# Conditioning products for two tiles at a time, x and result in one ring of four buffers, in a two-layer adapter kernel

## The chip, the cores and the metric

The kernel runs on one core of a Trainium2 chip. The metric is device time in microseconds (us), lower is better. The core has TensorE (in the rows PE, its weight loads PEld), VectorE (DVE), ScalarE (ACT), GpSimd (POOL) and SyncE (SP), which here issues every DMA. All engines run their own program and meet at semaphores.

## The reference

```python
def cond0(x, weights, condition):                 # 128 samples, 64 channels, 1024 columns
    return jnp.einsum('bct,bcd->bdt', x, weights[condition])     # one 64x64 matrix a sample
def ffn0(x, W_base, b_base, W_router, A, B):      # 8 experts of rank 16, best 2, scale 2
    probs = softmax(x @ W_router.T); top2, idx = top_k(probs, 2); top2 /= top2.sum(-1, keepdims=True)
    combine = einsum('nk,nke->ne', top2, one_hot(idx, 8))
    hw = einsum('nd,erd->ner', x, A) * combine[:, :, None]
    return x @ W_base.T + b_base + einsum('ner,eor->no', hw, B) * 2
def cond1(x, ids, W, b, A, B):                    # one of 32 adapters of rank 16 a sample
    return x @ W.T + b + einsum('bsr,bor->bso', einsum('bsd,brd->bsr', x, A[ids]), B[ids])
def ffn1(x, w, bias, s_in, s_w):                  # both operands rounded to fp8 first
    return einsum('ni,io->no', fp8(x / s_in), fp8(w / s_w)) * (s_in * s_w) + bias
x = x + ffn0(cond0(x, ...), ...)
x = x + ffn1(cond1(x, ...), ...)
```

## The kernel before

The 8192 rows are 64 tiles of 128 rows, two samples a tile. The kernel has two stages with a loop over the 64 tiles in each; every engine has its own copy of the loops, and the order of its instructions is the order in which the Python code writes them.

**Stage 1**, some 15 us a tile. TensorE works in three PSUM banks g = 0, 1, 2 (`bank_g`), eight k-steps of 128 rows in each; every float32 product is made of three matmuls with the operands split in a high and a low part (`st_h`, `st_l`, `w0h`, `w0l`), so a tile has 72 of them (lines 977 to 979). Bank 0 also holds the adapters' and the router's columns. Behind bank 1 stands the *conditioning product* of the next tile (`cond`, line 957): 16 matmuls with 64 rows and 32 columns of weights each, from `wpair` (two 64x64 matrices) and `xbuf` (the next tile's x) into `bank_f`. Behind bank 2 nine matmuls add the experts' part (lines 1004 to 1006), for which VectorE must have made `hwt` out of bank 0 (softmax, best two, a transpose, 12 small casts at line 317 with ScalarE doing 4 more). Then the next tile follows.

VectorE transposes the conditioned tile from `bank_f` to `bank_t` in two halves (`turn_y`, line 727), ScalarE rounds each half to `st_h` (`st_hi`, line 624) once TensorE has read the old one (`st_used`, raised at half and at the end of bank 2), and VectorE subtracts (`st_lo`, line 733) to `st_l`. It adds x and stores the result to `x1buf` (line 831) and a block-transposed copy to `x1_blocks` (line 840). GpSimd adds the bias row to `xbuf` (`add_bias`, line 547).

x and result have two buffers each (`xbuf`, `x1buf`). SyncE's order in a tile: first `feed(t)`, which for three pieces of the second stage's tables (40 pieces in all) waits for GpSimd's `split` (`pool_lo`), stores the two parts and loads the next piece; then `tile(t)`: wait for the result, store it, load x of tile t+2 and its two matrices (`load_cond`, with a value loaded from `ids0_sb` for each), store the four blocks. ScalarE and VectorE quantize one piece of `wq` in each of the tiles 2 to 33. TensorE's loop body is two tiles (tiles 2 to 61); the other engines write tiles 0 to 33 out.

Ahead of tile 0, 26 pieces of the stage's weights come in through 12 staging slots (8 in `wq`, 4 in `x1buf`) and are split by ScalarE and VectorE (lines 630, 743), which also serves tile 0's operands behind piece 1.

**Stage 2**, some 15 us a tile: the same three banks with 72 matmuls (lines 1030 to 1032), three for the adapters' second part and the bias (line 1075, operand `b_stack`), and 16 bf16 matmuls for the quantized product of the tile before (line 1040). ScalarE and VectorE make `st_h` and `st_l` of the transposed tile read back from DRAM (`turned_hi`, line 676; `turned_lo`, line 882). `turned_hi` waits for `main_done`, the end of bank 2 of the tile before. The bias rows are split on chip between the stages (`bias_h`, `bias_l`) and copied into both `b_stack`.

## Time and profile before

| | us |
|---|---|
| median of 3 runs | 2020.85 (2020.4 to 2025.44) |
| profiled execution, its own time | 2019.35 |
| its span | 2017.5 |
| TensorE busy | 1983.1 (98%) |
| VectorE busy | 1490.1 (74%) |
| GpSimd busy | 517.5 (26%) |
| ScalarE busy | 393.9 (20%) |

The span is the stretch that the trace covers, all times in its rows count from its start. Stage 1 ends near 1014 us, stage 2 takes the rest. In the rows an engine's "idle before" is followed by what released it. PEclk is the clock granted to TensorE, 1.00 for 2.4 GHz and 0.50 for 1.2 GHz.

### The profile page before, as it was taken

Reading aid. Unit: us, or ns where it says so; the run is one execution under the profiler, and the core shown is the slowest. Engines: PE = TensorE matmul, PEld = TensorE weight load, DVE = VectorE, ACT = ScalarE, POOL = GpSimd, SP = SyncE. Lnnn points to the kernel's source line nnn. Section 1 sums busy time; section 2 is a strip of 40 time slices with the busy share of each in tenths; the row PEclk is TensorE's granted clock in tenths of the full one; section 3 lists DMA queues with packets and bytes.
Section 4 is the critical chain, followed back from the end, with each engine's and each line's share of the span. In section 5 each row is a group of like instructions: output and inputs, shape, how many; then the busy total and the mean of one; then the engine's idle time right before and its main releaser. Section 6 shows DMA issues by size and latency. Waiting matters only on the chain.

```text
span 2017.5 us, 38464 instructions
## 1 busy us (share of the span) xinstructions
PE 1983.1 (98%) x13056; PEld 1802.5 (89%) x13056; DVE 1490.1 (74%) x3882; ACT 393.9 (20%) x1084; POOL 517.5 (26%) x469
## 2 busy tenths in 40 slices
PE   6899999999999999999999999999999999999998
PEld 5889999999999999999988888888888888888887
DVE  6887877777766666666657777777777777777777
ACT  3112111111211111111112121212121222122211
POOL 3655411111111111111112222322232223222222
PEclk8999999999999999999999999999999999999999
DMA  7764443343333333333455566566656665665564
GB/s 241 226 192 140 135 122 107 104 126 116 101 111 110 98 97 116 106 96 113 123 162 151 163 166 161 152 168 164 163 148 173 160 161 149 173 159 161 155 171 111
DMA packets 220202, 289.93 MB, mean 144 GB/s; under 512 B 97795, under 2 KB 169477, under 8 KB 220166
## 3 DMA queue, kind: packets, MB, share of 16 engines
q1 hardware_dynamic: 220166, 289.56, 50.7%
q14 instruction: 27, 0.22, 0.0%
q8 instruction: 9, 0.15, 0.0%
HBM read 163.62 MB, written 109.05 MB: 135 GB/s over the span
## 4 chain that ended last, share of the span: by engine, by line
PE 93%; SPq 2%; DMA 2%; POOL 1%; DVE 1%; issue 0%; ACT 0%; DVEq 0%; ACTq 0%
PE bank_g L977 13%; PE bank_g L1032 12%; PE bank_g L979 12%; PE bank_g L978 12%; PE bank_g L1031 12%; PE bank_g L1030 12%; PE bank_f L1040 11%; PE bank_f L957 3%; PE bank_g L1075 1%; PE bank_g L1005 1%; PE bank_g L1006 1%; PE bank_g L1004 1%; DMA raw<-b 1%; DMA raw<-a 1%; POOL w1h L557 1%; POOL w1l L559 1%
## 5 line engine op out<-in xcount | busy, mean ns | idle before, releaser
L977 PE MATMUL bank_g<-w0h,st_h 128*128 128x384 f32 (+1 forms) x1536 | 529.7, 345 | 10.4 <-DMA wpair<-wc 6.5
L978 PE MATMUL bank_g<-w0l,st_h 128*128 128x384 f32 (+1 forms) x1536 | 520.7, 339 | 0.0
L979 PE MATMUL bank_g<-w0h,st_l 128*128 128x384 f32 (+1 forms) x1536 | 520.6, 339 | 0.0
L1030 PE MATMUL bank_g<-w1h,st_h 128*128 128x352 f32 x1536 | 506.1, 329 | 4.0 <-DVE st_l L882 4.0
L1032 PE MATMUL bank_g<-w1h,st_l 128*128 128x352 f32 x1536 | 496.7, 323 | 0.0
L1031 PE MATMUL bank_g<-w1l,st_h 128*128 128x352 f32 x1536 | 495.8, 323 | 0.0
L882 DVE TENSOR_TENSOR st_l<-xbuf,st_h 128x512 fp32r<-128x512 f32 x128 | 212.8, 1703 | 183.9 <-ACT st_h L676 183.9
L977 PEld LDWEIGHTS bank_g<-w0h,st_h 128*128 128x128 f32 x1536 | 289.5, 188 | 41.2 <-issue 26.1
L547 POOL TENSOR_TENSOR xbuf<-xbuf,b_base_sb 128x1024 f32<-128x1024 f32 x64 | 154.4, 2412 | 654.0 <-PE bank_f L957 640.4
L1030 PEld LDWEIGHTS bank_g<-w1h,st_h 128*128 128x128 f32 x1536 | 289.2, 188 | 11.9 <-DVE st_l L882 4.6
L1031 PEld LDWEIGHTS bank_g<-w1l,st_h 128*128 128x128 f32 x1536 | 289.0, 188 | 1.6
L978 PEld LDWEIGHTS bank_g<-w0l,st_h 128*128 128x128 f32 x1536 | 289.7, 189 | 0.0
L979 PEld LDWEIGHTS bank_g<-w0h,st_l 128*128 128x128 f32 x1536 | 289.6, 189 | 0.0
L1032 PEld LDWEIGHTS bank_g<-w1h,st_l 128*128 128x128 f32 x1536 | 289.4, 188 | 0.0
L1040 PE MATMUL bank_f<-wq,rqt 128*128 128x512 bf16 x1008 | 228.6, 380 | 0.1
L601 POOL TENSOR_TENSOR obuf<-x1buf,bias_sb 128x1024 f32<-128x1024 f32 x64 | 176.8, 2763 | 153.2 <-DMA out<-obuf 153.2
L582 POOL TENSOR_TENSOR w1h<-raw,ones 128x128 fp32r<-128x128 f32 x128 | 48.7, 402 | 585.5 <-DMA raw<-a_split 546.9
L1040 PEld LDWEIGHTS bank_f<-wq,rqt 128*128 128x128 bf16 x1008 | 93.8, 98 | 112.4 <-issue 0.4
L317 DVE CAST hwt<-hw_parts 32x64 fp32r<-32x64 f32 x768 | 150.4, 196 | 11.8
L733 DVE TENSOR_TENSOR st_l<-bank_t,st_h 128x512 fp32r<-128x512 f32 x128 | 87.7, 686 | 79.3 <-ACT st_h L624 78.9
L831 DVE TENSOR_TENSOR x1buf<-bank_g,xbuf 128x384 f32<-128x384 f32 (+1 forms) x192 | 91.9, 506 | 73.5 <-PE bank_g L1006 73.4
L615 ACT ACTIVATE ht<-h_parts 32x32 fp32r<-32x32 f32 x192 | 43.8, 228 | 488.0 <-DVE h_parts L907 486.5
(79 smaller groups left out, 1988.8 us busy)
## 6 DMA issues: line engine op xcount, KB each, us to landing
xbuf<-x SPq DMA_DIRECT2D x64, 512.0 KB, 3.9
x_scratch<-x1buf SPq DMA_DIRECT2D x64, 512.0 KB, 2.9
x1t_scratch<-x_blocks SPq DMA_DIRECT2D x256, 128.0 KB, 2.3
xbuf<-x1t_scratch SPq DMA_DIRECT2D x64, 512.0 KB, 3.6
x1buf<-x_scratch SPq DMA_DIRECT2D x64, 512.0 KB, 5.1
out<-obuf SPq DMA_DIRECT2D x64, 512.0 KB, 2.7
b_stack<-b_split SPq DMA_DIRECT2D x384, 64.0 KB, 3.6
raw<-a_split SPq DMA_DIRECT2D x128, 128.0 KB, 4.2
```

Of the source, the lines that this page charges most:

```text
L317: last = engine_move(hwt[32 * q:32 * q + 32, :, 32 * a:32 * a + 32], hw_parts[32 * a:32 * a + 32, :, 32 * q:32 * q + 32])
L547: pool.tensor_tensor(xbuf[:, b, :], xbuf[:, b, :], b_base_sb[:, :], ALU.add).then_inc(xb_done, 1)
L601: pool.tensor_tensor(obuf[:, b, :], x1buf[:, b, :], bias2_sb[:, :], ALU.add).then_inc(x1b_done, 1)
L831: dve.tensor_tensor(x1buf[:, b, cols], bank_g[:, g, G0_OUT[g]:G0_WIDTH[g]], xbuf[:, b, cols], ALU.add).then_inc(x1_done[g], 1)
L882: last = dve.tensor_tensor(turned(st_l[:, :], h), in_blocks(xbuf[:, b, :], h), turned(st_h[:, :], h), ALU.subtract)
L977: pe.matmul(to, st_h[:, rows], w0h[:, k, cols], start=(k == 0), stop=False)
L978: pe.matmul(to, st_h[:, rows], w0l[:, k, cols], start=False, stop=False)
L979: last = pe.matmul(to, st_l[:, rows], w0h[:, k, cols], start=False, stop=(k == KC - 1))
L1030: pe.matmul(to, st_h[:, rows], w1h_k[:, k, cols], start=(k == 0), stop=False)
L1031: pe.matmul(to, st_h[:, rows], w1l_k[:, k, cols], start=False, stop=False)
L1032: last = pe.matmul(to, st_l[:, rows], w1h_k[:, k, cols], start=False, stop=(k == KC - 1))
L1040: last = pe.matmul(bank_f[:, h, :], rqt[:, k * P:(k + 1) * P], wq[:, k, h * HALF:(h + 1) * HALF], start=(k == 0), stop=(k == KC - 1))
```

## The change

1. TensorE makes the conditioning products of two tiles in one block of 32 matmuls, in every second tile only; the results lie in a PSUM tensor of four banks (`bank_y`). `bank_t` shrinks to one bank, so that the second half is transposed only when the first half has been split.
2. `xbuf` and `x1buf` become `ring`, four buffers; the result takes the place of its x. x of tile t+4 is loaded when the store of result t has landed (`x1_stored`). The loop bodies of TensorE, VectorE, GpSimd and SyncE are four tiles; 36 tiles (TensorE: 4) are written out before them.
3. SyncE does `tile(t)` first and `feed(t)` behind it, with two table pieces a tile. The bias row is one more table piece (41), split by GpSimd and read back from DRAM.
4. At the start x of tile 1 and 2 is loaded between the weight pieces, the bias row `b_base` and x of tile 3 behind them; two of the staging slots lie in `x1_blocks`.
5. Between the stages: VectorE makes `turned_lo` of tile 0 half by half around the last result; in all of stage 2 `turned_hi` goes by `st_used`, half by half; GpSimd fills the adapter columns of tile 1 before it waits for the result and `bias2`.

```diff
-POOL_PIECES_A_TILE = 3
+POOL_PIECES_A_TILE = 2
+RING = 4
+UNROLLED = -(-PREP_TILES // RING) * RING
+def pairs_to(t):
+    return (t + 1) // 2 + 1
...
+        y_of = (bank_y[:, 2:4, :], bank_y[:, 0:2, :])
+        bank_f, bank_l = bank_y[:, 0:2, :], bank_y[:, 2:4, :]
...
                     if n == KC - 1:
-                        sp.dma_start(b_base_sb[:, :], b_base.partition_broadcast(P)).then_inc(b_base_loaded, 16)
...
-                        sp.dma_start(xbuf[:, 1, :], x_t[1]).then_inc(x_loaded[1], 16)
-                        load_cond(1, 1)
+                    if n in (KC + KC // 2 - 1, 2 * KC - 1):
+                        r = 1 if n < 2 * KC - 1 else 2
+                        sp.dma_start(ring[:, r, :], x_t[r]).then_inc(x_loaded[r], 16)
+                        load_cond(r, r)
+                sp.dma_start(b_base_sb[:, :], b_base.partition_broadcast(P)).then_inc(b_base_loaded, 16)
+
+                sp.wait_ge(w0_lo, len(w0_units))
+                sp.dma_start(ring[:, RING - 1, :], x_t[RING - 1]).then_inc(x_loaded[RING - 1], 16)
...
-                    if more:
-                        sp.dma_start(xbuf[:, b, :], x_t[bass.ds(t + 2, 1)].rearrange("a p n -> (a p) n"))\
-                          .then_inc(x_loaded[b], 16)
-                        load_cond(t + 2, b)
...
+                    if more:
+
+                        sp.wait_ge(x1_stored, 16 * (t + 1))
+                        sp.dma_start(ring[:, r, :], x_t[bass.ds(t + RING, 1)].rearrange("a p n -> (a p) n"))\
+                          .then_inc(x_loaded[r], 16)
+                        load_cond(t + RING, r)
...
-                for t in range(PREP_TILES):
+                for t in range(UNROLLED):
+                    tile(t, t % RING, True)
                     feed(t)
-                    tile(t, t % 2, True)
...
-                        act.wait_ge(main_done, t)
                     for h in range(2):
+
+                        act.wait_ge(st_used[h], TILES + t)
...
+                def cond(pair):
+
+                    for r, _ in pair:
+                        for s in range(2):
+                            cols = slice(s * D // 4, (s + 1) * D // 4)
+                            for q in range(4):
+                                for j in range(PER_TILE):
+                                    rows = slice(j * CH, (j + 1) * CH)
+                                    last = pe.matmul(y_of[r % 2][32 * q:32 * q + 32, j, cols],
...
                     last.then_inc(y_ps, 1)
...
+                cond_in([(0, 1)], None)
+                cond([(0, 1)])
+                tile(0, False, [(1, 1), (2, 1)])
+                tile(1, True, ())
+                tile(2, True, [(3, 1), (0, 2)])
+                tile(3, True, ())
+                with pe.Fori(RING, TILES - 2 * RING + 1, RING) as i:
```

On TensorE, at the conditioning product inside tile 1 before the change (lines 977 to 979 are the three matmuls of a k-step of bank 1 and then bank 2), there stands:

```order
L977 MATMUL bank_g<-w0h,st_h 128x384 [waits st_ps1,wc_loaded0,x_loaded0]
L978 MATMUL bank_g<-w0l,st_h 128x384
L979 MATMUL bank_g<-w0h,st_l 128x384
L957 MATMUL bank_f<-xbuf,wpair 32x256 x16
L977 MATMUL bank_g<-w0h,st_h 128x384 [waits x1_done2]
```

In the changed program tile 1 has no such block. Tile 2 has one of twice the length (lines 990 to 992 and 970 are the new numbers of the same matmuls):

```order
L990 MATMUL bank_g<-w0h,st_h 128x384 [waits wc_loaded0,x_loaded0,st_ps1,wc_loaded3,x_loaded3]
L991 MATMUL bank_g<-w0l,st_h 128x384
L992 MATMUL bank_g<-w0h,st_l 128x384
L970 MATMUL bank_y<-ring,wpair 32x256 x32
L990 MATMUL bank_g<-w0h,st_h 128x384 [waits x1_done2]
```

The block moved from every tile to every second one, with x and matrices of two tiles awaited at once. On VectorE, behind the 12 small casts of tile 0, there stands before the change:

```order
L317 CAST hwt<-hw_parts 32x2x32 x11
L727 STREAM_TRANSPOSE bank_t<-bank_f 128x512 [waits y_ps]
L727 STREAM_TRANSPOSE bank_t<-bank_f 128x512
L733 TENSOR_TENSOR st_l<-bank_t,st_h 128x512 [waits hi_done0]
L831 TENSOR_TENSOR x1buf<-bank_g,xbuf 128x256 [waits acc_ps0,xb_done]
L733 TENSOR_TENSOR st_l<-bank_t,st_h 128x512 [waits hi_done1]
```

In the changed program, at the same place:

```order
L327 CAST hwt<-hw_parts 32x2x32 x11
L740 STREAM_TRANSPOSE bank_t<-bank_y 128x512 [waits lo_done1,y_ps]
L746 TENSOR_TENSOR st_l<-bank_t,st_h 128x512 [waits hi_done0]
L740 STREAM_TRANSPOSE bank_t<-bank_y 128x512 [waits lo_done0]
L849 TENSOR_TENSOR ring<-bank_g,ring 128x256 [waits acc_ps0,xb_done]
L746 TENSOR_TENSOR st_l<-bank_t,st_h 128x512 [waits hi_done1]
```

The second transpose moved behind the first subtraction. On SyncE, behind the end of tile 0, there stands before the change (`TENSOR_LOAD` and what follows it is the loading of an index for `load_cond`; the six rows before these are table pieces that wait for `pool_lo`):

```order
L397 DMA a_split<-w1h 128x4x128 [waits pool_lo]
L397 DMA a_split<-w1l 128x4x128
L370 DMA raw<-a 128x4x128
L410 DMA x_scratch<-x1buf 128x1024 [waits x1_done2]
L413 DMA xbuf<-x 128x1024
L348 TENSOR_LOAD ids_sb
```

In the changed program:

```order
L426 DMA x_scratch<-ring 128x1024 [waits x1_done2]
L432 DMA x1t_scratch<-x_blocks 32x4x256 [waits blocks_done]
L432 DMA x1t_scratch<-x_blocks 32x4x256 x3
L437 DMA ring<-x 128x1024 [waits x1_stored]
L358 TENSOR_LOAD ids_sb
```

The table pieces moved behind the tile's own transfers, and the load of x behind the result's store and the blocks.

## Rows read from the trace of the kernel before

**Rows 1.** The page: busy time and its share of the span.

```profile
PE 1983.1 (98%) x13056; PEld 1802.5 (89%) x13056; DVE 1490.1 (74%) x3882; ACT 393.9 (20%) x1084; POOL 517.5 (26%) x469
```

**Rows 2.** Stages: window, its length, busy by engine, PEclk, DMA share, GB/s.

```profile
600.00:800.00 200.00, 200.00 (x1475) 189.43 (x1474) 127.45 (x444) 33.82 (x105) 31.38 (x13) 1.00 0.34 104
1000.00:1200.00 200.00, 195.00 (x1142) 174.59 (x1141) 142.10 (x301) 39.46 (x102) 46.84 (x59) 0.99 0.58 162
...
35.70:41.80 6.10, 6.07 (x20) 6.10 (x21) 4.91 (x8) 1.19 (x2) 6.02 (x4) 0.50 0.73 194
...
1031.30:1035.20 3.90, 3.87 (x14) 3.87 (x15) 3.80 (x5) 0.00 (x0) 0.00 (x0) 0.56 0.84 308
```

**Rows 3.** TensorE in order of time: last matmuls of tiles 0, 5, 62, 63.

```profile
38.11 0.52 PE L1006 MATMUL bank_g<-b0h,hwt 128*128 128x384 f32 x1
...
125.41 0.34 PE L1006 MATMUL bank_g<-b0h,hwt 128*128 128x384 f32 x1
...
999.32 0.34 PE L1006 MATMUL bank_g<-b0h,hwt 128*128 128x384 f32 x1
...
1013.46 0.34 PE L1006 MATMUL bank_g<-b0h,hwt 128*128 128x384 f32 x1
```

**Rows 4.** TensorE in order of time, around one conditioning product.

```profile
501.75 0.34 PE L979 MATMUL bank_g<-w0h,st_l 128*128 128x384 f32 x1
502.02 1.09 PE L957 MATMUL bank_f<-xbuf,wpair 64*32 64x256 f32 x32
503.04 0.44 PE L977 MATMUL bank_g<-w0h,st_h 128*128 128x384 f32 x1
503.32 0.34 PE L978 MATMUL bank_g<-w0l,st_h 128*128 128x384 f32 x1
```

**Rows 5.** Groups by line: busy, mean ns; then that block's records in flight in 0.05 us.

```profile
L957 PE MATMUL bank_f<-xbuf,wpair 64*32 64x256 f32 x2048 | 71.7, 390 | 6.3 <-DMA wpair<-wc 6.3
...
502.25:502.30 0.05, 0.05 (x15) 1.00 0.90 307
```

**Rows 6.** Waits on SyncE and TensorE up to 130 us: total, times, longest.

```profile
SPq L397 <- POOL w1l L559: 31.1, 7, 6.7
...
PE bank_g L1004 <- DVE hwt L317: 6.8, 1, 6.8
PE bank_g L977 <- DMA wpair<-wc: 6.5, 4, 3.0
```

**Rows 7.** TensorE in tile 4; SyncE's largest wait in the whole span.

```profile
100.33 0.69 PE L977 MATMUL bank_g<-w0h,st_h 128*128 128x384 f32 x1 [3.03 <-DMA wpair<-wc]
...
SPq L410 <- DVE x1buf L831: 455.5, 58, 9.3
```

**Rows 8.** VectorE in one tile of the steady state.

```profile
503.35 1.31 DVE L727 STREAM_TRANSPOSE bank_t<-bank_f 128x512 f32<-128x512 f32 x2
506.13 0.69 DVE L733 TENSOR_TENSOR st_l<-bank_t,st_h 128x512 fp32r<-128x512 f32 x1 [1.47 <-ACT st_h L624]
507.99 0.42 DVE L831 TENSOR_TENSOR x1buf<-bank_g,xbuf 128x256 f32<-128x256 f32 x1 [1.17 <-PE bank_g L1006]
```

**Rows 9.** VectorE, the 12 casts to hwt: tile 0, then a steady tile.

```profile
31.87 3.71 DVE L317 CAST hwt<-hw_parts 32x64 fp32r<-32x64 f32 x12
...
501.04 2.39 DVE L317 CAST hwt<-hw_parts 32x64 fp32r<-32x64 f32 x12
```

**Rows 10.** TensorE's idle stretches between the stages.

```profile
1016.30 0.43 PE L1030 MATMUL bank_g<-w1h,st_h 128*128 128x352 f32 x1 [2.50 <-DVE st_l L882]
...
1029.09 0.74 PE L1075 MATMUL bank_g<-b_stack,ht 98*128 98x320 f32 x3 [1.00 <-DMA b_stack<-bias_l]
...
1031.33 0.43 PE L1030 MATMUL bank_g<-w1h,st_h 128*128 128x352 f32 x1 [1.50 <-DVE st_l L882]
```

**Rows 11.** Instruction queue, window 50:100 (packets, MB, share); a DMA of 16 KB, us to landing.

```profile
q8 instruction: 3, 0.05, 0.5%
...
wpair<-wc SPq DMA_DIRECT2D x4, 16.0 KB, 2.1
```

More of the change, by code:

```diff
@@ L774, in quantize_weight, with tile @@
                     dve.tensor_tensor(to, to, wq_nan, ALU.add).then_inc(wq_step, 1)
-                def tile(t, b, stored, blocks, more, piece=None):
+                def tile(t, r, next_pairs, blocks, more, piece=None):
                     n = t + 1
@@ L973, in bank @@
                             pe.wait_ge(w0_lo, w0_need[g] - KC + k + 1)
[L974 to L975 removed]
+                        if pair and k == KC - 1:
+                            cond_in(pair, n)
                         rows = slice(k * P, (k + 1) * P)
@@ L983, in bank, with tile @@
                     return last
-                def tile(t, b, loads, prior, more):
+                def tile(t, prior, pair):
                     n = t + 1
@@ L992, in tile @@
                             pe.wait_ge(x1_done[g], t)
-                        last = bank(g, n, prior, *((loads, 1 - b) if g == 1 and more else ()))
+                        last = bank(g, n, prior, pair if g == 1 else ())
                         if g == 0:
                             last.then_inc(h_ps, 1)
-                        if g == 1 and more:
-                            cond(1 - b)
+                        if g == 1 and pair:
+                            cond(pair)
                     for e in range(2):
```

226 lines of the change are left out of this document (108 added, 118 removed).

## The prediction

> **What bounds the kernel now.** I read the page first: TensorE is busy 98% of the span, the next engine 74% [rows 1]. So the end moves only by what TensorE does or waits for, and the views that count are those of TensorE's idle time and of its order in time. The table of stages shows the steady state of stage 1 without idle time, 200.00 of 200, and 195.00 between 1000 and 1200 us, where the stages meet [rows 2]. The last matmuls of four tiles then measure tiles: tiles 6 to 62 take (999.32 - 125.41)/57 = 15.33 us each; tile 63, the only one without a conditioning product, takes 1013.46 - 999.32 = 14.14; tiles 1 to 5 take 125.41 - 38.11 = 87.3, which is 10.7 more than five steady ones [rows 3]. So there are three sources of gain: the conditioning product (62 x 1.19 us in tiles 1 to 62), the start (10.7), and the seam between the stages. The sum is made against the profiled execution's own 2019.35 us; the median of the runs shown is 1.5 above it.
>
> **The conditioning product.** It costs a tile 15.33 - 14.14 = 1.19 us. The order in time says what of. Main matmuls start 14.14/81 = 0.175 apart; the block starts 0.27 behind the last of them, the next main one 1.02 behind the block's start, and the one after 0.28 later [rows 4]. The 32 records of the block lie in 1.09 us, one takes 0.39, and 15 are in flight 0.23 to 0.28 us after its start [rows 4, 5]. So they come in four waves of 8 (2 row halves by 4 column quarters of the array), the last starting 1.09 - 0.39 = 0.70 after the first, less 0.05 for the issue within a wave: 0.65/3 = 0.22 from wave to wave. The next main matmul starts only when the last wave has nearly run out. A second product right behind the first adds four waves, 4 x 0.215 = 0.86 us, and saves one entry and one exit, 0.33. Bounds: it adds no less than 0.70, the starts of one block, and no more than the whole 1.19.
> Tiles 1 to 63 before hold 62 products: 73.8 us. After, the blocks stand in tiles 0, 2, ..., 62; in tiles 1 to 63 these are 30 pairs and one single: 31 x 1.19 + 30 x 0.86 = 62.7. That is -11.1 us: 9.9 by fewer entries and exits, and one product less since tile 0 takes it on. In tile 0 TensorE waits 6.8 us for hwt anyway [rows 6], so the 0.86 there are covered; without that cover they would be +0.9.
>
> **The second transpose, which moved behind the first subtraction.** VectorE's first subtraction starts at 506.13 and takes 0.69, so the transpose (1.31 for two, 0.68 for the second) now runs from 506.85 to 507.53, in the 1.17 us in which VectorE waited for TensorE before 507.99 [rows 8]. ScalarE rounds the second half only when TensorE is done with bank 2, which is no earlier. Cost nothing; 0.46 us of cover are left ahead of line 831, whose result releases bank 0 of the next tile. In tiles without a block everything on TensorE behind bank 1 comes 1.19 earlier against VectorE's chain to hwt; hwt is ready at 501.04 + 2.39 = 503.43 [rows 9], and line 1004, 23 matmuls behind the one at 503.32 [rows 4], starts at 503.32 + 23 x 0.175 = 507.3, so 3.9 us of slack shrink to 2.7. Cost nothing.
>
> **The ring.** x of tile t+4 now waits for the store of result t, and is needed by a block that stands two tiles later or more. SyncE sat 455.5 us in 58 tiles waiting for a result, 7.9 a tile [rows 7]; its work in a tile is the other 7.4 of 15.3, and the new wait for a store of 512 KB, a few us, fits in what is left. It is hidden, with a tile as margin.
>
> **The start.** SyncE waited seven times for GpSimd's pieces, 31.1 us, before it got to a tile's own loads, and TensorE then waited for the matrices `wpair`, 6.5 us in four stalls [rows 6]; the longest, in tile 4, is 3.03 us [rows 7]. The change puts the pieces behind, and loads four tiles ahead. So the 10.7 us should go, but for what the clock takes: from 35.7 to 41.8 us TensorE ran at 0.50, which is 1.2 GHz, behind the 6.8 us of waiting in tile 0 [rows 2, 6]. That wait stays, so tile 1 still loses about half of the 3.4 us behind 38.4, 1.7. Net -9.0. If two tiles still wait for late loads it is -5.
> Tile 0 itself: the 12 casts took 3.71 against 2.39 in the steady state [rows 9], while GpSimd split table pieces; these now come later, -1.3. Against that the last weight piece is issued later, since SyncE puts x and both matrices of one more tile ahead of it. VectorE's chain to hwt starts behind the last piece; I give 0.8 of the 1.3 back: -0.5, with -3 and +2 as ends.
>
> **The seam.** Three idle stretches, 2.50 + 1.00 + 1.50 = 5.0 us [rows 10], and a clock of 0.56 behind the last, which costs about 1.7 more [rows 2]. `turned_lo` of tile 0 no longer stands behind the last transpose, the bias rows come from DRAM, and `turned_hi` starts at half of bank 2: all three releasers come earlier. What is late next: the six DMAs to `b_stack` of tile 0, which stand behind the same result as before, and bank 0 of stage 2's tile 1, which ScalarE must read out before it is written, with no bf16 matmuls to cover that yet. I take 1.2 of the 6.7 us for both: -5.5, with -3.5 if the clock falls once again. In stage 2 proper TensorE has no idle time to give back, and `turned_hi` earlier by half a bank releases nobody: 0.
>
> **TensorE's longer program.** Its loop body grows from two tiles to four, and 4 tiles stand ahead of it. Here one rule speaks against the change. The rows show three packets of 16 KB on an instruction queue between 50 and 100 us [rows 11], which I read as TensorE's code, about one a tile; from 100 to 1000 us, in the loop, that queue is silent. So the old body, two packets long and so in up to three, with the one ahead of it, is held without a fetch: four packets at least. The new body is four long, so five or six with its ends and the one ahead. Whether that many are held no row shows. I take nothing, since nothing in the trace marks an edge between four and six. The Trainium skill, page "Runtime: NRT & Kernel Launch", section "Instruction fetch mechanics", says two things: that TensorE's instruction memory holds 128 KiB, by which the sum stays as it is, and that it is only two lines, a taken branch out of which stalls for a fetch, by which it would grow at each of the 13 jumps back. The silent queue speaks against two lines.
>
> **Sum.** -11.1 - 9.0 - 0.5 - 5.5 = -26.1: 2019.35 - 26.1 = 1993.3 for a profiled run, and 1.5 more for the median, **1995 us**. The ends of the terms: -11.1 becomes -1.2 if the pair saves nothing and -15.3 with 0.72 for the second product; the others -5, +2 and -3.5 on one side, -10.7, -3 and -7.2 on the other. Not all fall on one side: 1989 to 2003 for this case.
>
> **The rivals.**
> *The pair saves no entry* (each product runs out before the next, since weights for new rows are loaded): 30 x 0.33 = +9.9, 2005. Against it: waves with other weights already follow each other at 0.22 within a block. Chance 0.08.
> *VectorE becomes the bound*: its chain through one `bank_t` releases bank 0 late. From a delay of 0.46 us on each tile pays the excess; two `add_bias` in a row beside it are what could bring it. With 0.3 us on 63 tiles +19, 2014. For it: the cover is the smallest in the kernel. Chance 0.07.
> *SyncE stays late at the start*: a table piece waits for GpSimd, the store behind it, and TensorE again for `wpair`: +8, 2003. Chance 0.09.
> *The jump back stalls* (slower): the loop's first packet is no longer held. Price of one: a DMA of the same 16 KB lands 2.1 us after its issue [rows 11], so 2 to 3 us; 13 jumps give +26 to +39, 2021 to 2034. It decides from 2.0 us a jump on. Chance 0.06.
> The forecast itself has 0.70.
>
> **Chances.** A difference of 0.3%, 6 us, is about what a measurement of this kernel can tell from none. Faster by more: all but the last rival and part of the second, 0.92; within: 0.03; slower: 0.05. The range 1988 to 2006 holds the forecast's own and the two rivals near 2004.
>
> **What the changed profile would show.** The block's record count 64 in every second tile, with next main matmul about 1.89 us behind its start; tiles alternating 14.14 and 16.2 us; tiles 1 to 5 without waits for `wpair`; the stretch 1000 to 1200 with less than 2 us idle; no packets on the 16 KB queue in the loop. The prediction is wrong if TensorE waits on `x1buf`'s line in every tile, or if a gap stands at every fourth tile's start.

## Result: 10.7 us faster, where 26 were predicted

| | before | after |
|---|---|---|
| median | 2021.18 us (5 runs, 2020.4 to 2025.44) | 2010.44 us (5 runs, 2009.63 to 2013.28) |
| profiled execution, its span | 2017.5 us | 2008.1 us |

The ratio is 0.9945, 95% interval 0.9932 to 0.9958. The median lies 4.4 us above the upper end of the predicted range. The page of the changed kernel, its busy times and the costliest group (at its end the idle time before it and what ended most of that):

```profile
PE 1973.0 (98%) x13056; PEld 1809.6 (90%) x13056; DVE 1437.2 (72%) x3881; ACT 400.1 (20%) x1083; POOL 494.7 (25%) x471
...
L990 PE MATMUL bank_g<-w0h,st_h 128*128 128x384 f32 (+1 forms) x1536 | 526.0, 342 | 10.3 <-DVE ring L849 5.4
```

The shares look as in [rows 1]. New is the releaser in the group's last column: TensorE's bank 0 waits for `ring L849`, VectorE's addition that reads a bank and writes the result (line 831 before). To see where the 26 us went, the span is cut at four events, as in [rows 3]: the last matmul of tile 0, of tile 11 and of tile 63, and the last of the three LoRA matmuls (line 1075 before, 1095 after) of stage 2's third tile. "Steady" is 11 x 15.33 = 168.6 us before, and 6 x 14.14 + 5 x 16.20 = 165.8 with pairs.

| | before | after | moved | predicted |
|---|---|---|---|---|
| tile 0 ends at | 38.11 | 40.12 | +2.0 | -0.5 |
| tiles 1 to 11, above steady | 10.6 | 13.0 | +2.4 | -9.0 |
| fewer entries and products: 2.79 in tiles 1 to 11, 8.29 in tiles 12 to 63 (796.08 to 787.79) | | | -11.1 | -11.1 |
| end of stage 1 to the third LoRA block | 46.84 | 44.60 | -2.2 | -5.5 |
| rest of stage 2, to the end | | | -0.4 | 0 |
| sum before rounding, against spans of 2017.5 and 2008.1 | | | -9.4 | -26.1 |

So one term was exact and three failed. TensorE's waits of over 0.1 us between 40 and 215 us in the changed kernel (total, times, longest):

```profile
PE bank_g L990 <- DVE ring L849: 5.4, 6, 1.4
PE bank_g L1017 <- DVE hwt L327: 3.7, 3, 2.1
```

and the two longest up to 41 us, the first at the start of the program (it ended at 6.28 us, and at 6.31 before the change), the second at the end of tile 0:

```profile
PE bank_y L970 <- DMA wpair<-wc: 6.3, 1, 6.3
PE bank_g L1017 <- DVE hwt L327: 6.3, 1, 6.3
```

The four stalls on `wpair` of [rows 6] are gone from the tiles behind tile 0, as the change intended; in their place stand six on the result of VectorE and three on hwt. The longest of these three is in tile 10, which took 20.63 us; behind it the clock was 0.50 (1.2 GHz) from 202 to 204 us. VectorE and GpSimd tell why hwt was late there. First VectorE in order of time (start, us, what), a quantizing step and the casts:

```profile
188.34 2.50 DVE L787 TENSOR_TENSOR wq_val<-wq_val,wq_pow 128x256 f32<-128x256 f32 x1
190.87 0.42 DVE L789 TENSOR_TENSOR wq<-wq_val,wq_pow 128x256 bf16<-128x256 f32 x1
...
194.92 6.59 DVE L327 CAST hwt<-hw_parts 32x64 fp32r<-32x64 f32 x12
```

and GpSimd in the same stretch:

```profile
188.12 2.44 POOL L562 TENSOR_TENSOR ring<-ring,b_base_sb 128x1024 f32<-128x1024 f32 x1
194.80 1.01 POOL L572 TENSOR_SCALAR w1h<-raw 128x320 fp32r<-128x320 f32 x1 [4.25 <-DMA raw<-w1t]
195.90 0.91 POOL L574 TENSOR_TENSOR w1l<-raw,w1h 128x320 fp32r<-128x320 f32 x1
196.78 1.08 POOL L572 TENSOR_SCALAR w1h<-raw 128x352 fp32r<-128x352 f32 x1
197.95 0.99 POOL L574 TENSOR_TENSOR w1l<-raw,w1h 128x352 fp32r<-128x352 f32 x1
198.91 2.34 POOL L562 TENSOR_TENSOR ring<-ring,b_base_sb 128x1024 f32<-128x1024 f32 x1
```

Line 787 starts 0.22 us behind the bias addition and ends 0.28 behind its end, and the row behind it, of nearly the same shape, takes 0.42. The 12 casts take 6.59 us where [rows 9] has 2.39, while GpSimd works without a gap from 194.80 to 201.25.

Such collisions were there before the change too. VectorE between 40 and 215 us in the kernel before (busy, mean ns), where the same cast takes 186 ns and the same quantizing step some 290 ns undisturbed:

```profile
L317 DVE CAST hwt<-hw_parts 32x64 fp32r<-32x64 f32 x132 | 26.1, 198 | 2.0
...
L766 DVE TENSOR_SCALAR wq_pow<-wq_pow 128x256 f32<-128x256 f32 x9 | 7.4, 822 | 0.3
```

Added up over VectorE's instructions of this stretch, the time above the undisturbed duration of the same instruction is, as an estimate from the two traces, some 21 us before and 23 after. Before the change TensorE waited for none of it. So two things are new: the casts of tile 10 lie beside five GpSimd instructions in a row, and, as the experiments show, the other tiles have less room for a late hwt.

The pair itself was as forecast, one block of 64 records; TensorE around it, in order of time:

```profile
500.71 1.96 PE L970 MATMUL bank_y<-ring,wpair 64*32 64x256 f32 x64
502.59 0.44 PE L990 MATMUL bank_g<-w0h,st_h 128*128 128x384 f32 x1
```

The next main matmul starts 1.88 us behind the block's start; 1.89 was forecast. From tile 12 on, tiles alternate between 14.14 and 16.20 us. At the seam, TensorE's waits between 1010 and 1050 us:

```profile
PE bank_y L1062 <- DMA rqt<-rq: 2.3, 1, 2.3
PE bank_g L1049 <- ACT val L705: 0.5, 1, 0.5
```

The stalls of [rows 10] shrank from 5.0 us to 0.5, but a new one of 2.3 came, and behind it the clock fell (window, length, busy by engine, PEclk):

```profile
1034.60:1038.00 3.40, 3.40 (x10) 1.21 (x9) 3.37 (x2) 0.00 (x0) 2.91 (x2) 0.50 0.00 0
```

SyncE's issues in order of time show the cause of the late `rqt`. VectorE finished rq at 1027.8 (its last step starts at 1027.12 and takes 0.69), and SyncE came to turn it only at 1031.15, behind the loads of tile 2's adapters:

```profile
1026.42 0.34 SPq L464 DMA_DIRECT2D raw<-a_split  x1
1026.86 1.34 SPq L471 DMA_DIRECT2D b_stack<-b_split  x3
1028.95 0.35 SPq L464 DMA_DIRECT2D raw<-a_split  x1
1029.76 1.29 SPq L471 DMA_DIRECT2D b_stack<-b_split  x3
1031.15 1.36 SPq L510 DMA_TRANSPOSE rqt<-rq  x1
```

### The profile page after: what moved, and what is told of

Its sections match the earlier page's. It is cut to its first block, busy times and chain, and to the rows that moved or that the text cites. A ratio compares the mean times of both kernels' runs of the same rounds, so it can differ in the third digit from the quotient of the medians.

```text
span 2008.1 us, 38332 instructions
## 1 busy us (share of the span) xinstructions
PE 1973.0 (98%) x13056; PEld 1809.6 (90%) x13056; DVE 1437.2 (72%) x3881; ACT 400.1 (20%) x1083; POOL 494.7 (25%) x471
## 4 chain that ended last, share of the span: by engine, by line
PE 91%; DVE 5%; issue 1%; DMA 1%; SPq 1%; ACT 1%; POOL 0%; DVEq 0%; ACTq 0%; POOLq 0%
PE bank_g L990 12%; PE bank_g L992 12%; PE bank_g L991 12%; PE bank_g L1051 12%; PE bank_g L1050 12%; PE bank_g L1049 12%; PE bank_y L1062 11%; PE bank_y L970 3%; PE bank_g L1095 1%; PE bank_g L1019 1%; PE bank_g L1017 1%; PE bank_g L1018 1%; DVE hwt L327 1%; DVE wq_pow L785 0%; DVE x_blocks L860 0%
## 5 line engine op out<-in xcount | busy, mean ns | idle before, releaser
L771 DVE TENSOR_TENSOR st_l<-ring,st_h 128x512 fp32r<-128x512 f32 x128 | 142.3, 1112 | 228.5 <-ACT st_h L688 228.4
L562 POOL TENSOR_TENSOR ring<-ring,b_base_sb 128x1024 f32<-128x1024 f32 x64 | 152.8, 2402 | 564.3 <-PE bank_y L970 534.3
L1062 PE MATMUL bank_y<-wq,rqt 128*128 128x512 bf16 x1008 | 230.3, 382 | 2.3 <-DMA rqt<-rq 2.3
L617 POOL TENSOR_TENSOR obuf<-ring,bias_sb 128x1024 f32<-128x1024 f32 x64 | 154.9, 2420 | 181.7 <-DMA out<-obuf 172.8
L1062 PEld LDWEIGHTS bank_y<-wq,rqt 128*128 128x128 bf16 x1008 | 93.7, 98 | 116.3 <-DMA rqt<-rq 2.6
L688 ACT ACTIVATE st_h<-ring 128x512 fp32r<-128x512 f32 x128 | 80.9, 632 | 340.8 <-PE bank_g L1051 337.2
L640 ACT ACTIVATE st_h<-bank_t 128x512 fp32r<-128x512 f32 x128 | 76.7, 599 | 292.6 <-PE bank_g L992 168.9
```

Of the source, the lines that this page charges most:

```text
L562: pool.tensor_tensor(ring[:, r, :], ring[:, r, :], b_base_sb[:, :], ALU.add).then_inc(xb_done, 1)
L617: pool.tensor_tensor(obuf[:, b, :], x1buf[:, b, :], bias2_sb[:, :], ALU.add).then_inc(x1b_done, 1)
L771: dve.tensor_tensor(turned(st_l[:, :], h), in_blocks(xbuf[:, b, :], h), turned(st_h[:, :], h), ALU.subtract).then_inc(lo_done[h], 1)
L1062: last = pe.matmul(bank_f[:, h, :], rqt[:, k * P:(k + 1) * P], wq[:, k, h * HALF:(h + 1) * HALF], start=(k == 0), stop=(k == KC - 1))
```

## Experiments

The theory to be tested: certain instructions of VectorE stand still while a GpSimd instruction between SBUF operands runs; hwt and with it the result come late; and `bank_t` with one bank leaves less room for that than before. Rivals: SyncE's order alone, the quantizing work itself, loads that are late in another place. All kernels start from the changed one unless said otherwise. Every ratio is against the kernel before, on the same chip.

| | median, us | ratio (95% interval) | tile 0 ends | tiles 1 to 11 above steady | third LoRA block |
|---|---|---|---|---|---|
| changed kernel | 2010.44 | 0.9945 (0.9932 to 0.9958) | 40.12 | 13.0 | 44.60 |
| splits behind the casts | 2004.63 | 0.9918 (0.9905 to 0.9932) | 40.21 | 8.0 | 43.53 |
| pieces ahead of the tile | 2011.1 | 0.9942 (0.9927 to 0.9958) | 40.79 | 14.1 | 44.96 |
| single products | 2024.57 | 1.0013 (1.0004 to 1.0023) | 39.49 | 12.1 | 44.54 |
| third x behind the weights | 2008.19 | 0.9933 (0.9918 to 0.9948) | 38.55 | 12.8 | 44.83 |
| bias and splits behind the casts, pieces ahead | 1996.73 | 0.9869 (0.9855 to 0.9883) | 39.12 | 1.8 | 44.52 |
| the same, pieces behind | 1999.21 | 0.9882 (0.9867 to 0.9897) | 38.82 | 2.7 | 42.21 |
| single products, two banks | 2015.99 | 0.9959 (0.9946 to 0.9972) | 40.23 | 7.2 | 45.42 |
| rq ahead of the loads | 2014.37 | 0.9952 (0.9939 to 0.9965) | 40.61 | 15.8 | 46.71 |
| bias beside the casts, loop only | 2029.04 (one run) | | 40.91 | 15.2 | 42.37 |
| seam in a third order | 1993.14 | 0.9851 (0.9836 to 0.9866) | 38.13 | 0.7 | 40.61 |
| the same, third x behind the weights | 1990.9 | 0.984 (0.9827 to 0.9854) | 37.66 | 0.0 | 40.77 |

The last three columns are measured in one profiled execution of each kernel, as in the table above, and kernels whose edit does not reach a stretch show how far they spread: tile 0 ends at 40.12 to 40.91 and the excess is 13.0 to 15.8 us in the changed kernel, "rq ahead of the loads" and "bias beside the casts, loop only"; the third LoRA block comes at 42.2 to 45.4 us in the nine kernels with the changed kernel's seam. Differences within these spreads show nothing.

### Splits behind the casts

```diff
                     add_bias(pairs_to(t), t % RING)
+                    if pool_pieces(t):
+                        pool.wait_ge(hwt_done[1], t + 1)
                     for n in pool_pieces(t):
```

> The changed kernel, but in each of the first 21 tiles GpSimd splits its table pieces only when VectorE's casts to hwt of that tile are done. Theory A (GpSimd's splits and bias additions fall on VectorE's quantizing and casts, and hold up its chain to hwt): the 12 casts take 2.39 us in every one of tiles 1 to 11, the quantizing steps 0.25 to 0.43 each, and tiles 1 to 11, which took 12.8 us above the pattern of 14.14 and 16.20, come down to at most 3 above it. Time 2000 to 2002 us against 2010.4. Rival B (the loads of SyncE are late, or the one-bank bank_t makes the chain too long by itself): tiles 1 to 11 stay 10 us or more above the pattern, 2009 to 2012.

Measured 2004.63, between the spans of the two theories. The excess fell from 13.0 to 8.0 us, where theory A had at most 3; tile 10 fell from 20.63 to 17.26 us, and the clock dip in it went. Casts and quantizing steps on VectorE between 40 and 215 us (busy, mean ns), first in the changed kernel, then with the wait:

```profile
L327 DVE CAST hwt<-hw_parts 32x64 fp32r<-32x64 f32 x131 | 29.3, 223 | 2.0
...
L785 DVE TENSOR_SCALAR wq_pow<-wq_pow 128x256 f32<-128x256 f32 x9 | 10.6, 1176 | 0.3
```

```profile
L327 DVE CAST hwt<-hw_parts 32x64 fp32r<-32x64 f32 x132 | 24.6, 186 | 2.0
...
L787 DVE TENSOR_SCALAR wq_pow<-wq_pow 128x256 f32<-128x256 f32 x9 | 11.6, 1287 | 0.3
```

The casts are back at their undisturbed 186 ns; the quantizing step (same instruction, its line moved by two) is not, at 1287 where an undisturbed one takes 290 (0.29 us). Tiles 4, 6 and 8 stayed at 17.87 us. So half of the theory was shown, and the other half pointed at the bias addition.

### Pieces ahead of the tile

```diff
-                    tile(t, t % RING, True)
                     feed(t)
+                    tile(t, t % RING, True)
```

> The changed kernel with one part undone: feed(t) stands ahead of tile(t) again, still two pieces a tile. Theory A: what counts is when GpSimd works, and here the next pieces come in the middle of a tile instead of near its end, so their splits stand between the casts and the end of bank 2 or on the casts; the excess of tiles 1 to 11 changes by several us either way, I expect 4 to 10 instead of 12.8: 2002 to 2008. TensorE does not wait for wpair, since the ring is loaded tiles ahead. Rival B (SyncE's lateness is what stops TensorE): TensorE waits for wpair come back, and the time is 2015 or more.

Measured 2011.1: nothing. Tile 1 came 18.09 us long and the excess was 14.1, within the spread. Both theories missed here: the excess did not move, and no wait for `wpair` came back behind tile 0. So with four buffers and two pieces a tile, SyncE's order of these two does not matter; it is not the order that cured the four stalls on `wpair`. The prediction had taken the 31.1 us of SyncE's waits in [rows 6] for the cause of the whole excess; at most the 6.5 us of waits for `wpair` came of them.

### Single products

```diff
 def pairs_to(t):
-    return (t + 1) // 2 + 1
+    return t + 1
...
-                tile(0, False, [(1, 1), (2, 1)])
-                tile(1, True, ())
-                tile(2, True, [(3, 1), (0, 2)])
-                tile(3, True, ())
+                tile(0, False, [(1, 1)])
+                tile(1, True, [(2, 1)])
+                tile(2, True, [(3, 1)])
+                tile(3, True, [(0, 2)])
```

(and the same in the loop; GpSimd's and VectorE's counts follow `pairs_to`)

> The changed kernel, with the conditioning product of one tile in every tile as before (ring of four, one-bank bank_t and the order of SyncE stay). By the prediction's first term tiles settle at 15.33 us in place of 14.14 and 16.20, and the steady tiles 12 to 61 cost 50 x (15.33 - 15.17) = 8 us more. If the excess of the first tiles stays as it is, 2018 to 2020. Theory A adds that the slack ahead of hwt is 1.2 us more in every second tile, so that some of the excess goes: down to 2014. If the pair's gain were nothing: 2010.

Measured 2024.57, above both expectations. Pairs are worth 14.1 us here (2024.57 - 2010.44), more than their 11.1, because the rest of the change costs something with single products: tiles 30 to 35 took 15.57 to 16.0 us, and every fourth one from 39 to 59 15.57 to 15.8, where the kernel before had 15.33 in nearly all. No GpSimd split is near these tiles, but the bias addition is. VectorE and GpSimd in one of them, in order of time:

```profile
520.61 4.63 DVE L327 CAST hwt<-hw_parts 32x64 fp32r<-32x64 f32 x12
522.37 2.41 POOL L562 TENSOR_TENSOR ring<-ring,b_base_sb 128x1024 f32<-128x1024 f32 x1 [13.58 <-PE bank_y L968]
```

The addition starts ahead of the last of the twelve casts, which takes 2.43 us instead of 0.19; twelve tiles from 490 to 940 us have one such cast. So it is the same collision, with neither a split nor, in the later tiles, a quantizing step near, and this kernel has no room for it.

### Third x behind the weights

```diff
-                    if n in (KC + KC // 2 - 1, 2 * KC - 1):
+                    if n in (KC + KC // 2 - 1, len(w0_units) - 1):
```

(the second insertion of x, matrices and `b_base` now stands behind all weight pieces)

> The changed kernel, with x and matrices of tile 2 loaded behind the last of the 26 weight pieces. Theory: tile 0 ended at 40.1 us (38.1 before the change), because these loads stand ahead of the last ten weight pieces, VectorE waited 2.3 and 1.1 us for pieces, and the bias row's addition on GpSimd then fell on the router's first step (1.54 us against 0.22). With them behind, negmax of tile 0 stands near 28.5 to 29.5 instead of 30.8, and tile 0 ends at 37 to 39. The later tiles keep their excess. 2007 to 2010. Rival (the two-step transpose at the start is what costs): no change of negmax's time, tile 0 ends at 40 or later, as TensorE's block comes later.

Measured 2008.19. Tile 0 ended at 38.55 instead of 40.12, as expected. TensorE's waits up to 41 us:

```profile
PE bank_y L970 <- DMA wpair<-wc: 6.4, 1, 6.4
PE bank_g L990 <- DMA wpair<-wc: 6.3, 1, 6.3
```

The first of these is the one at the start of the program. The wait for hwt of tile 0 is no longer among them; the second wait for matrices has taken its place, and ended at 28.36 us. `negmax` came at 27.76, sooner than expected, and the bias addition held the step behind it and the casts up all the same (line 819 took 2.22 us instead of 0.17, the casts 3.06). So the DMA order in front of tile 0 has a share in its end, 1.6 us here. It is not to be added to what the bias addition costs there: with that behind the casts and the loads as in the changed kernel, tile 0 ends at 39.12, 38.82 and 38.13 (three kernels below).

### Bias addition and splits behind the casts, pieces ahead of the tile

```diff
-                    add_bias(pairs_to(t), t % RING)
+                    if pool_pieces(t):
+                        pool.wait_ge(hwt_done[1], t + 1)
+                    add_bias(pairs_to(t), t % RING)
...
-                    tile(t, t % RING, True)
                     feed(t)
+                    tile(t, t % RING, True)
```

> In the tiles that carry table pieces GpSimd does the bias addition and the splits only when the casts of hwt are done, and SyncE serves the pieces ahead of its tile work again. Theory A (the excess of tiles 1 to 11, 12.8 us in the changed kernel and 8.0 us with only the splits held back, is VectorE's casts and quantizing steps standing still while a GpSimd instruction runs, the bias addition among them): tiles 4, 6 and 8 fall from 17.87 to near 16.2 us, the excess of tiles 1 to 11 falls to 3 us or less, median 1998 to 2002. Rival B (the late x1 of those tiles comes from the quantizing work itself, 1.7 us more on VectorE and ScalarE than the one-bank chain leaves room for): tiles 4, 6 and 8 stay at 17.8, median 2003 to 2006. Rival C (the wait for the matrices of wpair comes back since the pieces stand ahead again): waits on wpair of over 2 us in tiles 2 to 6, median 2005 to 2009.

Measured 1996.73. TensorE's waits between 40 and 215 us are one:

```profile
PE bank_g L992 <- DVE ring L851: 0.2, 1, 0.2
```

Tiles 2 to 11 are at 14.14 and 16.20, but for tile 8 at 16.34; of the 13.0 us 1.8 are left, nearly all in tile 1. GpSimd does the same instructions, and the quantizing work is unchanged, so rival B falls; no wait for `wpair` came, so C falls. By the estimate used above, VectorE's time lost to collisions in this stretch is some 7 us instead of 23, none of it on the casts. The median lies 1.3 us below theory A's span.

### The same with the pieces behind the tile

> As the kernel at 1996.73 (bias addition and splits behind the casts, pieces served ahead of the tile), but SyncE serves the pieces behind the tile's transfers as the changed kernel does. Theory A (GpSimd's bias addition beside the quantizing steps and casts is the whole of what was left, 8.0 us of excess in tiles 1 to 11 with only the splits held back): tiles 4, 6 and 8 at 16.2 to 16.4 us, median 1996 to 1998.5. Rival B (SyncE's order has a share: x and pieces arrive at other times and the splits land on the next tile's quantizing steps): tiles 4, 6 and 8 at 17 us or more, median 2000 to 2004.

The diff is the first half of the one above. Measured 1999.21, 0.7 us above theory A's span, with tiles 4, 6 and 8 at 16.26 to 16.35 us as it said. Only tile 10, at 17.21, keeps a trace of SyncE's order. The kernels' intervals (0.9867 to 0.9897 and 0.9855 to 0.9883) overlap, so no difference between the two is shown. So the place of GpSimd's work is the cause; where SyncE serves the pieces decides some 1 us in tile 10.

### Bias addition beside the casts, in the loop only

```diff
                     for r in range(RING):
+                        pool.wait_ge(hw_lo_done, i + r + 1)
                         add_bias(half + pairs_to(r), r)
```

> In the loop of tiles 36 to 63 GpSimd's bias addition waits for the first of the casts behind hwt, so that it runs beside the others and nothing else of GpSimd's work is there. Theory A (a GpSimd addition and a VectorE instruction between SBUF operands exclude each other for their whole time): the small casts of these tiles rise from 186 ns of mean to over 280 ns since one of the twelve waits for the addition's end, 1.5 to 2.5 us a tile on that line; the transposes and subtractions out of PSUM keep their durations to 5%. Rival B (they share bandwidth): many casts are a little longer, none over 0.6 us. Tile times: by A 14.14 and 16.2 us stay or rise by up to 1.5 us where x1 becomes late, profiled time 2010 to 2035.

This moves one GpSimd instruction a tile onto the casts, in tiles 36 to 63, with no split and no quantizing near. VectorE between 640 and 960 us, first the changed kernel, then this one:

```profile
L327 DVE CAST hwt<-hw_parts 32x64 fp32r<-32x64 f32 x252 | 47.0, 186 | 3.9
L740 DVE STREAM_TRANSPOSE bank_t<-bank_y 128x512 f32<-128x512 f32 x43 | 31.2, 726 | 7.5 <-PE bank_y L970 6.8
```

```profile
L327 DVE CAST hwt<-hw_parts 32x64 fp32r<-32x64 f32 x242 | 90.7, 375 | 3.7
L741 DVE STREAM_TRANSPOSE bank_t<-bank_y 128x512 f32<-128x512 f32 x40 | 28.9, 721 | 0.7
...
641.78 4.57 DVE L327 CAST hwt<-hw_parts 32x64 fp32r<-32x64 f32 x12
```

Twelve casts of one tile take 4.57 us instead of 2.39: 2.18 more, and the mean gives the same, (375 - 186) x 12 = 2.27. The shortest, median and longest cast of that stretch in this run tell how it is spread:

```profile
L327 DVE CAST hwt<-hw_parts x242: 182/187/2406, 641.8 to 958.7; 32x64 fp32r<-32x64 f32 x121
```

One cast a tile, 21 in all, takes 2.28 to 2.41 us, and the other 221 take 182 to 193 ns. GpSimd's addition is not slower (the changed kernel, then this one):

```profile
L562 POOL TENSOR_TENSOR ring<-ring,b_base_sb 128x1024 f32<-128x1024 f32 x21 | 49.9, 2397 | 281.4 <-PE bank_y L970 281.4
```

```profile
L562 POOL TENSOR_TENSOR ring<-ring,b_base_sb 128x1024 f32<-128x1024 f32 x21 | 50.2, 2392 | 282.4 <-DVE hw_parts L835 282.4
```

So it is a full stop of the cast that comes second, not shared bandwidth, which would have lengthened many casts a little (rival B). The transposes out of PSUM are not stopped, and that is to be read from the changed kernel, since here no addition lies beside one. There two additions in a row do (VectorE and GpSimd in order of time):

```profile
654.44 0.73 DVE L740 STREAM_TRANSPOSE bank_t<-bank_y 128x512 f32<-128x512 f32 x1 [0.65 <-PE bank_y L970]
654.48 4.75 POOL L562 TENSOR_TENSOR ring<-ring,b_base_sb 128x1024 f32<-128x1024 f32 x2 [25.58 <-PE bank_y L970]
658.08 0.73 DVE L740 STREAM_TRANSPOSE bank_t<-bank_y 128x512 f32<-128x512 f32 x1
```

The transposes take 0.73 us beside them and 0.71 to 0.73 elsewhere, and the subtraction between them, with one operand in PSUM, 0.69 as elsewhere. The block transpose of line 860, from SBUF to SBUF, is not stopped either: 1245 ns on average in tiles 1 to 11 of the changed kernel, where GpSimd runs beside most of them, and 1246 here, where nothing does.

The Trainium skill, page "SBUF — State Buffer", section "Who interferes with whom", says this: GpSimd's only ports are VectorE's second pair, taken for a whole instruction by whichever engine issues first while the other waits; a cast can take that pair too, in a two-port mode, and an instruction of VectorE with at most one SBUF input outside the two-port modes does not meet it. The trace agrees: the casts are stopped (186 to 375 ns on average) and the transposes are not (726 and 721). That these casts ran in such a mode no run here shows by itself.

The run gives the slack too. Tiles of 14.14 us stayed; those of 16.20 became 17.53. Of 2.2 us of delay in each tile, every second one lets 1.33 through, at the start of the tile behind the one without a block (TensorE's waits for the result there are 1.1 us each). So a tile without a block has about 1 us to spare between hwt and the result.

### Single products with two banks

```diff
-        bank_t = whole.enter_context(nc.psum_tensor("bank_t", [P, 512], F32))
-        bank_y = whole.enter_context(nc.psum_tensor("bank_y", [P, 4, 512], F32))
+        bank_t = whole.enter_context(nc.psum_tensor("bank_t", [P, 2, 512], F32))
+        bank_y = whole.enter_context(nc.psum_tensor("bank_y", [P, 2, 512], F32))
...
                         turn_y(n, r + 1, next_pairs, 0)
-                        st_lo(n, 0)
                         turn_y(n, r + 1, next_pairs, 1)
+                        st_lo(n, 0)
```

(on top of the kernel with single products; with pairs a second bank for `bank_t` would be the ninth of the kernel's PSUM banks, and that was not tried)

> Single conditioning products as in the kernel with products for one tile at a time (2024.57), and bank_t has two banks again, both halves transposed ahead of the first subtraction; ring, loads and pieces are as in the changed kernel. Theory A (the one-bank chain, in which the second half is transposed only behind the first subtraction, uses up VectorE's slack, so that any late hwt makes x1 late): the tiles of 15.57 to 16.0 us among tiles 31 to 59 go back to 15.33, the excess of tiles 1 to 11 falls by 3 us or more, median 2014 to 2020. Rival B (the chain has no part; the collisions with GpSimd alone make the excess): within 1.5 us of 2024.6.

Measured 2015.99, 8.6 us less than with one bank. The slow tiles among 30 to 59 are all at 15.33 again (tiles 12 to 63 take 795.79 us instead of 801.08), the excess of tiles 1 to 11 is 7.2 instead of 12.1. TensorE's waits between 40 and 215 us, one bank, then two:

```profile
PE bank_g L988 <- DVE ring L848: 5.4, 6, 1.4
PE bank_g L1015 <- DVE hwt L327: 3.0, 1, 3.0
```

```profile
PE bank_g L1014 <- DVE hwt L327: 2.9, 1, 2.9
PE bank_g L987 <- DVE ring L847: 1.6, 3, 0.7
```

The wait for hwt is untouched, that for the result falls by two thirds. The late tiles say the same: VectorE in one of them,

```profile
622.58 4.60 DVE L327 CAST hwt<-hw_parts 32x64 fp32r<-32x64 f32 x12
```

has its last cast beside the bias addition as with one bank, and TensorE waits nowhere between 600 and 960 us. So the second bank does not stop the collision, it absorbs it. Tiles 31 to 35 do not show this, since there the addition no longer falls on a cast.

### The seam: rq ahead of the loads, and a third order

```diff
 def tile(t, b, first, lag, more):
+    early = isinstance(t, int) and t == 1
+    if early:
+        sp.wait_ge(s_const, 32)
+        sp.wait_ge(rq_done, t)
+        turn_rq(rqt, range(KC)).then_inc(rqt_in, 16)
```

(the same three lines further down are left out for this tile)

> In tile 1 of stage 2 SyncE transposes rq of tile 0 before it loads the adapters' matrices of tile 2. Theory A (rqt is late, 2.29 us of TensorE's waiting at 1034.35, because SyncE issues the 16 loads for tile 2 first): the wait for rqt falls below 0.5 us, the clock dip behind it goes, the LoRA matmuls of the second stage's third tile come 4 us earlier, median 2006 to 2008. Rival B (rq is late on VectorE): the wait moves by less than 0.5 us and the median stays at 2010 to 2011. Rival C (the late loads of the adapters' matrices take the place of the wait): a wait on b_stack or slot_done of 2 us or more, median 2010 to 2013.

Measured 2014.37: rival C, 1.4 us above its span. The wait for `rqt` is gone, and the slot of adapter matrices is late:

```profile
1043.82 0.61 PE L1054 MATMUL bank_g<-w1h,st_h 128*128 128x352 f32 x1 [4.11 <-POOL w1l L603]
```

SyncE had waited for rq with the two loads of `raw` behind it (the loads of tile 2 are eight, not the 16 of the expectation). The third order takes those two first, then rq, then the six loads to `b_stack`, and starts from the kernel at 1996.73:

```diff
+                            for j in range(PER_TILE):
+                                load_a(both[j], 1 - b, j)
+                            sp.wait_ge(s_const, 32)
+                            sp.wait_ge(rq_done, t)
+                            turn_rq(rqt, range(KC)).then_inc(rqt_in, 16)
+                            for j in range(PER_TILE):
+                                load_b(both[j], 1 - b, j)
```

> As the kernel at 1996.73, and in tile 1 of stage 2 SyncE issues the two loads of adapter matrices first, then the transpose of rq, then the six loads into b_stack. Theory A (rqt is late only because those six loads, 2.6 us of issuing, stand before it, and the earlier try made the two matrix loads late): the wait for rqt (2.5 us) falls below 0.7 us, no clock dip behind it, no wait on w1l of over 0.5 us, third LoRA block 40.3 to 41 us behind the end of stage 1 (44.52 there), median 1992 to 1994. Rival B (the transpose itself, rq being ready only then): the block moves by less than 1.5 us, median 1995 to 1997. Rival C (b_stack or the next x1 becomes late instead): a new wait of over 2 us, median 1996 or more.

Measured 1993.14, the third LoRA block at 40.61, 3.9 us sooner than in the kernel that it starts from: theory A in all its parts. The waits of TensorE from 1000 to 1045 us:

```profile
PE bank_g L1063 <- ACT val L719: 0.5, 1, 0.5
PE bank_y L1076 <- DMA rqt<-rq: 0.2, 1, 0.2
```

### All together

The kernel with the third order at the seam, and x of the third tile behind all weight pieces as above.

> The same with x of the third tile and the first pieces loaded behind all weight pieces. Theory A (the start's DMA queue is worked off in order, so tile 0 ends 0.5 to 1.5 us sooner and the third x is still in time): last matmul of tile 0 at 37.6 to 38.6 us (39.12 in the kernel at 1996.73), tiles 1 to 11 unchanged, median 1991 to 1993.5. Rival B (x and matrices of the first pair become late instead): a wait for wpair of 2 us or more in the tiles 0 to 2 eats it, median within 1 us of the seam kernel or above.

Measured 1990.9, ratio 0.984 (0.9827 to 0.9854): 1.6% less than the kernel before, and 1.1% less than the changed one (0.984/0.9945). Tile 0 ends at 37.66. The median is 0.1 us below the span expected, since tile 1 fell too, from 14.74 to 14.13. The waits for `wpair` up to 41 us are 6.5, at the start of the program, and 5.4, in tile 0. The second is rival B's sign, though its time did not come: the wait takes the place of the one for hwt. It is now what sets the end of tile 0, since hwt is ready at 33.0 us and TensorE reads it at 36.4; what loading that pair sooner would bring was not tried.

## Why the prediction was wrong, step by step

- **The conditioning product, -11.1: right.** Measured 2.79 + 8.29 = 11.1. The next main matmul 1.88 us behind the block's start, with 1.89 forecast, refutes the rival that the pair saves no entry.
- **The start, -9.0: wrong, +2.4.** The step that failed is "So the 10.7 us should go". It took an excess of 10.7, of which 6.5 were seen as waits for `wpair`, for something that earlier loads cure. The change did cure these waits, by the four buffers or the fewer pieces (which of them, no run here separates) and not by SyncE's order. But 5.4 us of waits for the result and 3.7 for hwt came in their place. The prediction put no cost on GpSimd's instructions beside VectorE's: it used the collision in tile 0 (casts at 3.71 against 2.39 in [rows 9]) as a gain there, and did not ask where else such collisions lie (some 21 us of VectorE's time in tiles 1 to 11 already before) and what room the changed chain leaves for them. The two kernels with bias addition and splits behind the casts bring the excess to 2.7 and 1.8 us, and the best to 0.0: the term is to be had, with 1.7 of clock that the prediction had conceded as well.
- **The second transpose, nothing: wrong beside disturbed tiles.** "3.9 us of slack shrink to 2.7" counted only what hwt itself may be late. The chain behind it (transpose, rounding on ScalarE, subtraction, second transpose, then line 849) has to end as well before the next tile's bank 0, and it has about 1 us; the rival "VectorE becomes the bound" had 0.46 for it. Two banks saved 8.6 us with single products; in the steady tiles with pairs the cost is indeed nothing, 787.79 us in 52 tiles.
- **Tile 0, -0.5: wrong, +2.0,** at the upper end that was given. The 1.3 us of the casts came back (2.39). The weight pieces are later by more than the 0.8 allowed: `negmax` starts at 30.78 instead of 28.10. And the first bias addition, at 30.73, holds line 805 for 1.54 us instead of 0.23. Putting the x behind the weights gives 1.6 us back, holding the bias addition behind the casts 1.0 to 2.0, and both together 2.5.
- **The seam, -5.5: mis-sized, -2.2.** The first three releasers do come earlier, as forecast. "What is late next" named `b_stack` and bank 0, with 1.2 us for both. Bank 0, which ScalarE reads out, came to 0.5; the rest was `rqt`, held up on SyncE's queue by the loads of tile 2's adapters, 2.3 us of waiting and a clock at 0.50 for 3.4 us, and TensorE was idle for 2.8 us between 1000 and 1200 us where less than 2 was forecast. With the six loads to `b_stack` behind it the seam gives -6.2 (46.84 to 40.61).
- **TensorE's longer program, nothing: right.** In the changed kernel no packet of 16 KB starts between 139 and 951 us, and no gap stands at every fourth tile. So a loop of four tiles is held, if these packets are TensorE's code, as the prediction read them; the rival that the jump back stalls is refuted by the tile times alone.
- **The ring, nothing: right.** SyncE waits 218.7 us for results between 500 and 900 us, where it waited 222.8 before.
- **The rivals.** "VectorE becomes the bound" through one `bank_t`, with "two `add_bias` in a row beside it", had 0.07 and names the mechanism. It was placed in all 63 tiles, and stands in six of the first eleven, where splits and quantizing steps are; the prediction's own sign of being wrong, a wait on that line in every tile, did not come.

With all of it repaired the terms are -0.5, -10.6, -11.1, -6.1 and -0.4 (tile 0, start, product, seam, rest): -28.7 (the spans, 1989.0 and 2017.5, give -28.5), where -26.1 was predicted. That this lies near the forecast does not make the forecast right: it takes three further edits that the prediction did not have. The gains were there to be had, and the costs of the collisions and of the shorter slack were missing.

Tile 1 is 14.13 to 15.9 us long in the kernels with pairs other than "pieces ahead of the tile". The clock and a wait of 0.2 to 0.3 us at its start account for that to some 0.2 us: the clock is 0.50 for a stretch around or behind tile 0's long wait, and half of the part of this stretch that falls into tile 1 is added to its length. In the changed kernel the stretch goes from 34.4 to 41.3 us and tile 1 starts at 40.12; in the kernel with all together it goes from 27.7 to 31.2, inside tile 0, and tile 1 has its 14.13.

Open: how much of the excess is due to the one bank and how much to the new places of the additions and splits, with pairs (the two banks were tried with single products only). Leaving GpSimd's splits out altogether was not tried.

## What to carry to other kernels

When an edit moves work or takes slack away, list each GpSimd instruction between SBUF operands, find where it lies before and after, and charge what is left of it to the VectorE instruction that starts beside it, where that is a cast, a `tensor_scalar` or a `tensor_tensor` between SBUF operands; transposes and what reads a bank of PSUM went free here. A slack is the shortest one to the end of the whole chain behind the late operand, and not the one up to its first reader. An excess over the steady state is explained only up to the waits that the trace shows; the rest of it (here 4.2 of 10.7 us) has another cause, and is not to be counted as gained.

## What the hardware showed that was not expected

- A GpSimd instruction between SBUF operands stops a cast or an elementwise instruction of VectorE between SBUF operands until its own end (a cast of 0.19 us takes up to 2.45), and five of them in a row stretch the casts of a tile from 2.39 to 6.59 us. Transposes, and subtractions with an operand in PSUM, keep their time.
- A wait of like length in the same place may or may not bring the clock down. Behind 2.3 us of waiting for `rqt` TensorE ran at 0.50, 1.2 GHz, for 3.4 us in the changed kernel. With the splits behind the casts the wait was 2.9 us, and the clock stayed at 1.00, 2.4 GHz:

```profile
1030.00:1034.00 4.00, 3.94 (x19) 2.15 (x20) 3.93 (x3) 0.00 (x0) 3.91 (x2) 1.00 0.00 0
```

  With waits of 1.6 and 1.8 us the third LoRA block came at 42.37 and 42.21, some 2.3 us earlier than with 2.3 us and the dip; 0.6 of that is the wait, the rest the clock. A stall of this size thus costs up to 1.7 us more than it shows.
